# Edge loop on TensorE: a half's adjacency products before its weights, its scatter last

## The chip, the cores and the metric

The kernel runs on one core of a Trainium2 chip. The metric is the device time of one execution in microseconds (us); the median of three runs before the change is 2267.75 us (2266.25 to 2269.3).

## The reference, cut to what matters

The reference is two layers of a graph transformer over 1250 nodes of 512 features and 41250 edges (20000 in each direction and a loop at each node). The change lies in the stage that walks over the edges. For each edge, a small network turns 8 edge features into 512 weights (4 groups of 128), which multiply the features of the sending node and four edge attributes; the products are summed by receiving node. The second layer needs the adjacency matrix of the same edges.

```
tpw = h @ W_mlp4 / sqrt(64)              # h: hidden activations of the edge network
w1, w2, w3, w4 = jnp.split(tpw, 4, axis=-1)
s0 = x0[sender]; s1 = x1[sender]
y0 = edge_attrs[:, 0:1]; y1 = edge_attrs[:, 1:4]
p1 = w1 * s0 * y0
p2 = (w2 * s0)[:, :, None] * y1[:, None, :]
p3 = w3[:, :, None] * s1 * y0[:, None, :]
p4 = w4 * jnp.einsum('eum,em->eu', s1, y1) / SQRT3
msg0 = segment_sum(concatenate([p1, p4]), receiver)
msg1 = segment_sum(concatenate([p2, p3]), receiver)
...
out = segment_sum(h[src] * norm[:, None], dst)   # second layer: degree-normed adjacency times h
```

## The kernel before, in words

**Stages.** Everything is written out by hand, engine by engine, with semaphores between the engines; no scheduler moves anything. First come the edge network's hidden layers and the dense parts (to about 235 us of the span), then the edge loop (to about 856 us), then the expert network and the second layer.

**Blocks and halves.** Edges are sorted by receiver. The 1250 nodes are cut into 45 blocks (`NB`) of 28 nodes. A block takes one pass here, and a pass has four halves (`HALVES`, q = 0 to 3) of 2 x 128 edges: 45 x 4 = 180 halves. A half n does this:

- SyncE (SP) loads the hidden activations (L833) and the edge records (L843: indices and attributes of its 256 edges) four halves ahead. `record_load` waits until `hot_y`, `hot_low` and `hot_step` of half n have been built from the old record in that buffer (lines 838 to 842) before it loads the record of half n+4. L841 is its wait on `step_ready`, L842 that on `hot_y_ready`.
- GpSimd (POOL) builds `hot_y` of half n (L1071), then gathers the sender rows of half n+2 from DRAM with two indirect DMAs (L1041). Before these it waits for the record of half n+2 (`record_loaded`).
- VectorE (DVE) builds the one-hot tiles `hot` and `hot_low` (L1709, L1712), then multiplies the weights in PSUM by the gathered rows in three instructions (L1720, L1721, L1722); the last one increments `products_done`. Once a block it also turns the finished adjacency columns of an earlier block (L1698).
- ScalarE (ACT) builds `hot_step` of half n with two activations (L1243), the last of which increments `step_ready`. At a block's end it first waits for the last half's `scatter_done`, copies the block's two PSUM accumulators out (L1250 the messages, L1252 the adjacency), and only then builds the first `hot_step` of the next block; in between stands `block_start` (L1231) for the block after.
- TensorE (PE) runs per half, in this order: wait for `products_done` of n; weights of half n+2, four 64-row matmuls (`tile_weights`, L2367), the last of which increments `weights_done`; wait for `hot_y`; 20 scatter matmuls into the messages' PSUM bank, 10 for each of two groups of 128 edges (L2397); wait for `hot_low` and `hot_step`; two adjacency matmuls into the adjacency's bank (L2408), the last of which increments `scatter_done`.

Banks for messages and adjacency exist twice, for even and odd blocks, and are zeroed at a block's start by two matmuls (L2383, L2384). The order of TensorE's work is that of the Python code in `block_work`. ScalarE's order at a block's end is

```
s = block_steps_of(i * 2 + 1, 1)     # hot_step of the block's four halves
block_store(i * 2, 0)
block_start(i * 2 + 2, 0)
block_flush(i, 1, s)                 # waits for scatter_done of the last half
s = block_steps_of(i * 2 + 2, 0)
```

and the wait of a record's load is

```
sp.wait_ge(hot_low_ready, s * 4 + q + 1)
sp.wait_ge(step_ready, s * 4 + q + 1)
```

Of the kernel before, what the change touches and what calls it, by code (L numbers as in the profile page):

```python
# [44 lines left out]
def graph_block_kernel(nc, A, out):  # L45
# [6 lines left out]
    MUL = A["L0_gnn_W_up0"].shape[0]  # L52
# [33 lines left out]
    with ctx:  # L86
# [3 lines left out]
        def sem(name):  # L90
            return ctx.enter_context(nc.semaphore(name))
# [174 lines left out]
        hot_y = [edge_space2.take(2 * Y * GRAIN).rearrange("p (j y n) -> p j y n", j=2, y=Y) for q in range(HALVES)]  # L266
        hot_low = [edge_space2.take(P).bitcast(BF16).rearrange("p (j n) -> p j n", j=2) for q in range(HALVES)]
        hot_step = [edge_space2.take(NT * STEPS).bitcast(BF16).rearrange("p (j a n) -> p j a n", j=2, a=NT) for q in range(HALVES)]
# [20 lines left out]
        msg_psum = [psum[:, k, 0:3 * MUL] for k in range(2)]  # L289
        adj_psum = [psum[:, 2 + k, 0:NT * STEPS] for k in range(2)]  # L290
# [83 lines left out]
        hot_low_ready = sem("hot_low_ready")  # L374
        step_ready = sem("step_ready")
# [330 lines left out]
        def block_units(eng, b):  # L706

            return eng.value_load(span[0:1, 1, bass.ds(b, 1)], min_val=1, max_val=EDGE_UNITS)
# [11 lines left out]
        def next_step(eng, step):  # L720

            eng.reg_add(step, step, 1)
            return eng.snap(step, min_val=1, max_val=NB * EDGE_UNITS)
# [1433 lines left out]
        def _(pe):  # L2157
# [207 lines left out]
            def tile_weights(q):  # L2365
                for j in range(2):
                    last = nc.tensor.matmul(tile_w[q % 2][:, j, :], h3_slot[q][halves[j], :], w_mlp4[halves[j], :], start=True, stop=True)  # L2367
                last.then_inc(weights_done, 1)
# [7 lines left out]
            bands = [slice(g * GRAIN, (g + 1) * GRAIN) for g in range(4)]  # L2376
            step = step_counter(pe, "pe_step")

            def block_work(b, k):
                units = block_units(pe, b)  # L2380
                pe.wait_ge(msg_flushed, b + 1)
                pe.wait_ge(adj_flushed, b + 1)
                nc.tensor.matmul(msg_psum[k], zeros16[:, 0:P], zeros16[:, 0:3 * MUL], start=True, stop=False, skip_group_check=True)  # L2383
                nc.tensor.matmul(adj_psum[k], zeros16[:, 0:P], zeros16[:, 0:NT * STEPS], start=True, stop=False, skip_group_check=True)  # L2384
                with pe.Fori(0, units) as u:
                    s = next_step(pe, step)
                    for q in range(HALVES):
                        ahead = (q + 2) % HALVES
                        pe.wait_ge(products_done, s * 4 + q + 5)
                        pe.wait_ge(half_loaded[ahead], s * 16 + (q + 2) // HALVES * 16)  # L2390
                        tile_weights(ahead)
                        pe.wait_ge(hot_y_ready, s * 4 + q + 5)
                        for j in range(2):
                            p = prod[q][:, j, :, :]

                            def scatter(g, y, cols, of):
                                nc.tensor.matmul(msg_psum[k].rearrange("p (c u) -> p c u", u=MUL)[bands[g], cols, :],  # L2397
                                                 hot_y[q][:, j, y, :], p[:, of, :], start=False, stop=True, skip_group_check=True)

                            scatter(3, 0, slice(0, 3), slice(5, 8))  # L2400
                            scatter(0, 1, slice(0, 2), slice(1, 3))
                            scatter(1, 2, slice(0, 2), slice(1, 4, 2))
                            scatter(2, 3, slice(0, 2), slice(1, 5, 3))
                            scatter(0, 0, slice(2, 3), slice(0, 1))
                        pe.wait_ge(hot_low_ready, s * 4 + q + 5)
                        pe.wait_ge(step_ready, s * 4 + q + 5)
                        for j in range(2):
                            last = nc.tensor.matmul(adj_psum[k], hot_low[q][:, j, :], hot_step[q][:, j, :, :].rearrange("p a n -> p (a n)"),  # L2408
                                                    start=False, stop=True, skip_group_check=True)
                        last.then_inc(scatter_done, 1)  # L2410

            with pe.Fori(0, NB // 2) as i:
                for k in range(2):
                    block_work(i * 2 + k, k)
            block_work(NB - 1, 0)

            def transposes(key, pieces):
# [20 lines left out]
            for key in chain_order():  # L2438
# [9 lines left out]
                elif key[0] == "msgT1":  # L2448
# [4 lines left out]
                    for m, i in enumerate((1, 4, 6)):  # L2453
                        last = nc.tensor.matmul(out_b[:, D - P:], parts[i], ident[:, :], start=(m == 0), stop=(m == 2))
                    last.then_inc(full, 1)
                elif key[0] == "degree":
                    pe.wait_ge(consts_ready, 4 + NT - 1)
                    out_b, full = claim(pe, key)
                    for t in range(NT):
                        last = nc.tensor.matmul(out_b[:, t:t + 1], adj_sum[:, tile_cols[t]], ones_col[:, :], start=True, stop=True)  # L2460
# [4 lines left out]
                elif key[0] == "router_bias":  # L2465
# [3 lines left out]
                    for c in range(C):  # L2469
                        last = nc.tensor.matmul(out_b[:, 0:EX], routers_T[:, c, EX + PARTS + 1:EX + PARTS + 2].to_broadcast([P, P]),  # L2470
                                                routers_T[:, c, 0:EX], start=(c == 0), stop=(c == C - 1))
                    last.then_inc(full, 1)
                elif key[0] == "logits":
                    drained(pe, ("hT", key[1]))
                    out_b, full = claim(pe, key)
                    for c in range(C):
                        last = nc.tensor.matmul(out_b[:, 0:EX], xn_T[:, c, tile_cols[key[1]]], routers_scaled[:, c, :],
                                                start=(c == 0), stop=(c == C - 1))
                    last.then_inc(full, 1)
                else:  # L2480
# [5 lines left out]
                    def chunk(i):  # L2486
                        return msg_T[:, t % 2, i * P:i * P + P]

                    for c, (i0, i1) in enumerate(((0, 7), (4, 1), (5, 2), (6, 3))):
                        w = w_out[:, min(c, 1), :, :]  # L2490
                        nc.tensor.matmul(out_b[:, c * P:c * P + P], chunk(i0), w[:, 0, :], start=True, stop=False)
                        last = nc.tensor.matmul(out_b[:, c * P:c * P + P], chunk(i1), w[:, 1, :], start=False, stop=True)
# [8 lines left out]
                             start=False, stop=True, skip_group_check=True).then_inc(full, 1)  # L2501
# [22 lines left out]
            with pe.Fori(0, EX // 2) as i:  # L2524
                bounds = expert_bounds(pe, i)
                for a in range(2):
# [3 lines left out]
                    with pe.Fori(lo, hi) as t:  # L2530
# [14 lines left out]
                        for f in range(FC):  # L2545
                            pe.wait_ge(gelu_done, t * FC + f + 1)
                            for c in range(C):
                                last = nc.tensor.matmul(psum[:, f % UP_BANKS, 0:P], ew1[a][:, c, f * P:f * P + P], tile_T[:, c, :],  # L2548
                                                        start=(c == 0), stop=(c == C - 1))
# [13 lines left out]
            for s in range(NT):  # L2563
# [7 lines left out]
                for t, (out_b, full) in enumerate(open_banks):  # L2571
                    last = nc.tensor.matmul(out_b, adj_in[0:r, s, tile_cols[t]], z_lo[0:r, s, :], start=False, stop=(s == NT - 1))
# [34 lines left out]
            for f in range(HC):  # L2607
                pe.wait_ge(split_lo, lo_no["gw1", f])
                w_hi, w_lo = gw1_hi[f % 2], gw1_lo[:, :, f * P:f * P + P]
                for g, (g0, w) in enumerate(COLS):  # L2610
                    out_b, full = claim(pe, ("h1T", f, g))
                    for c in range(C):
                        for k, (lhs, rhs) in enumerate(((w_hi, ah_hi), (w_hi, ah_lo), (w_lo, ah_hi))):
                            last = nc.tensor.matmul(out_b[:, 0:w], lhs[:, c, :], rhs[:, c, g0:g0 + w],  # L2614
                                                    start=(c == 0 and k == 0), stop=(c == C - 1 and k == 2))
                    last.then_inc(full, 1)
            for t in range(NT):
                out_b, full = claim(pe, ("y2", t))
                pe.wait_ge(split_lo, lo_no["h1", t])
                for c in range(HC):  # L2620
                    if t == 0:
                        pe.wait_ge(split_lo, lo_no["gw2", c])
                    for k, (lhs, rhs) in enumerate(((h1_hi, gw2_hi[:, c, :]), (h1_lo, gw2_hi[:, c, :]), (h1_hi, gw2_lo[c][:, 0, :]))):
                        last = nc.tensor.matmul(out_b, lhs[:, t % 2, c, :], rhs,  # L2624
                                                start=(c == 0 and k == 0), stop=(c == HC - 1 and k == 2))
# [5 lines left out]
            for m in range(C):  # L2631
                pe.wait_ge(split_lo, lo_no["wk", m])
                w_hi, w_lo = w_k_hi[m], w_qk_lo[:, :, D + m * P:D + m * P + P]
                for g, (g0, w) in enumerate(COLS):
                    out_b, full = claim(pe, ("kT", m, g))
                    for c in range(C):
                        for k, (lhs, rhs) in enumerate(((w_hi, xn_hi), (w_hi, xn_lo), (w_lo, xn_hi))):
                            last = nc.tensor.matmul(out_b[:, 0:w], lhs[:, c, :], rhs[:, c, g0:g0 + w],
                                                    start=(c == 0 and k == 0), stop=(c == C - 1 and k == 2))
# [10 lines left out]
            for t in range(NT):  # L2650
                out_b, full = claim(pe, ("ek", t))
                r = rows(t)
                for c in range(C):
                    last = nc.tensor.transpose(out_b[0:r, c * P:c * P + P], ek_T[:, c, t * P:t * P + r], ident[:, :])
# [5 lines left out]
            for c in range(C):  # L2660
                for t in range(NT):
                    r = slice(0, rows(t))
                    last = nc.tensor.matmul(out_b[:, c * P:c * P + P], vx_rows[r, t, c * P:c * P + P],
                                            ek_rows[r, t, c * P:c * P + P], start=(t == 0), stop=(t == NT - 1))
# [36 lines left out]
            for key in ffn_order():  # L2701
# [7 lines left out]
                elif key[0] == "down":  # L2709

                    _, g, j = key
# [5 lines left out]
                    for k, (h, w) in enumerate(((shid_hi, w2_hi), (shid_lo, w2_hi), (shid_hi, w2_lo))):  # L2717
                        for i, (out_b, full) in enumerate(outs):
                            last = nc.tensor.matmul(out_b, h[0:r, g % 2, j, i * P:i * P + P], w[0:r, j % 2, :],  # L2719
                                                    start=(j == 0 and k == 0), stop=(j == SC - 1 and k == 2))  # L2720
# [10 lines left out]
                if key == ("route",):  # L2731
                    for c in range(C):
                        last = nc.tensor.matmul(out_b[0:1, 0:PARTS], mean_col[:, c:c + 1], routers_T[:, c, EX:EX + PARTS],
                                                start=(c == 0), stop=(c == C - 1))
                elif key == ("expert_w",):
                    nc.tensor.matmul(out_b[:, 0:SE], ones_col[0:1, :].to_broadcast([1, P]), expert_w[:, 0, :], start=True, stop=True)
                    last = nc.tensor.matmul(out_b[0:SE, SE:SE + 1], expert_w[:, 0, :], ones_col[0:1, :], start=True, stop=True)
                elif key == ("b2_mix",):
                    last = nc.tensor.matmul(out_b, expert_w_col[:, :].to_broadcast([SE, P]), expert_b2[0:SE, :], start=True, stop=True)
# [20 lines left out]
```

## Time and profile before

| | us |
|---|---|
| median of 3 runs (lowest, highest) | 2267.75 (2266.25, 2269.3) |
| time of the profiled execution | 2266.87 |
| its span, first to last instruction | 2264.9 |
| edge loop, 235 to 856 us | 621 |
| TensorE busy in all | 2060.1 (91%) |
| mean granted clock of TensorE | 0.972 |

The profile gives for each engine when each instruction ran and what it waited for. `PE` is TensorE's matmuls, `PEld` its weight loads, `SPq`, `ACTq` and `POOLq` are what the sequencers of those engines issue. A note in square brackets is the idle time of the engine before the instruction and what ended it; "issue" means that the profile shows no releaser. A matmul's end is modelled.

### The profile page before, as it was taken

To read this page: it belongs to the slowest core of one execution; us is meant where nothing else is said; L and a number is where in the kernel's file an instruction comes from. 1 tells how busy PE (TensorE), PEld (TensorE's weight loads), DVE (VectorE), ACT (ScalarE), POOL (GpSimd) and SP (SyncE) were. 2 spreads that over 40 slices of the span, in tenths; PEclk is the share of its full clock that TensorE was granted. 3 is DMA by queue.
4 is the path that set the end of the run, shared out by engine and by line. 5 is a ranking of instruction groups with operands and counts; after the bars stand their busy time and mean duration, and the time that the engine had idled before them with its cause. 6 is when DMAs were issued, how large, how long until landed. Compare 5 with 4: busy or idle time off the path is not lost.

```text
span 2264.9 us, 45107 instructions
## 1 busy us (share of the span) xinstructions
PE 2060.1 (91%) x13564; PEld 1487.3 (66%) x13565; DVE 1335.5 (59%) x2849; ACT 1040.0 (46%) x2316; POOL 618.2 (27%) x739
## 2 busy tenths in 40 slices
PE   7899888888888888799999999999599999889998
PEld 4444344344434337588888888888388888768886
DVE  3212788889888876655555555555612346664444
ACT  6531333333333332277777777777143223354443
POOL 2102677778777774300000000002100000000000
PEclk9999999999999998699999999999799999989999
DMA  6642566667676678355603420042700200310000
GB/s 217 220 164 85 151 188 186 188 185 191 187 190 190 181 210 317 136 194 197 260 19 117 156 79 19 19 167 85 260 10 10 84 19 19 107 43 10 10 10 18
DMA packets 157291, 288.52 MB, mean 127 GB/s; under 512 B 43533, under 2 KB 85270, under 8 KB 152615
## 3 DMA queue, kind: packets, MB, share of 16 engines
q1 hardware_dynamic: 111349, 158.80, 20.4%
q0 software_dynamic: 37552, 121.91, 18.7%
q10 hardware_dynamic: 8322, 6.89, 0.9%
q8 instruction: 44, 0.72, 0.1%
q14 instruction: 24, 0.20, 0.0%
HBM read 233.69 MB, written 53.85 MB: 127 GB/s over the span
## 4 chain that ended last, share of the span: by engine, by line
PE 60%; DVE 13%; issue 10%; DMA 9%; POOL 3%; ACT 3%; DVEq 1%; POOLq 1%; ACTq 0%; SPq 0%
PE psum L2548 14%; DMA big_b<-sender_table,wide 7%; PE psum L2686 6%; PE psum L2719 4%; PE psum L2538 4%; PE psum L2539 3%; PE psum L2540 3%; PE psum L2584 3%; PE psum L2593 3%; PE psum L2624 3%; PE psum L2614 2%; POOL big_b L1041 2%; DVE big_b L1721 2%; DVE big_b L1722 2%; PE psum L2266 2%
## 5 line engine op out<-in xcount | busy, mean ns | idle before, releaser
L1041 POOL DMA_INDIRECT big_b<-sender_table,wide x360 | 368.5, 1024 | 117.0 <-issue 84.2
L2397 PEld LDWEIGHTS psum<-big_b,wide 128*32 128x32 f32 x3600 | 166.2, 109 | 195.9 <-issue 134.3
L2367 PE MATMUL psum<-w_mlp,wide 64*128 64x512 f32 x728 | 206.9, 645 | 81.4 <-DVE big_b L1722 78.2
L2548 PEld LDWEIGHTS psum<-xn_T,big_b 128*128 128x128 f32 x2048 | 261.9, 191 | 21.1 <-issue 3.1
L2397 PE MATMUL psum<-big_b,wide 128*32 128x256 f32 (+2 forms) x3600 | 272.0, 390 | 0.8 <-POOL wide L1071 0.8
L2548 PE MATMUL psum<-xn_T,big_b 128*128 128x128 f32 x2048 | 265.0, 275 | 0.0
L1250 ACT ACTIVATE wide<-psum 128x384 f32<-128x384 f32 x45 | 22.1, 490 | 393.3 <-PE psum L2408 369.0
L1896 DVE TENSOR_TENSOR w_lo<-wide,w_hi 128x512 fp32r<-128x512 f32 x184 | 127.4, 692 | 117.9 <-ACT w_hi L1342 117.9
L2538 PE MATMUL psum<-w_hi,hid_hi 128*128 128x512 f32 x368 | 175.8, 478 | 9.5 <-DVE w_lo L1896 7.2
L1243 ACT ACTIVATE wide<-wide 128x290 bf16<-128x290 f32 x360 | 158.6, 527 | 41.9 <-PEq L2370 37.2
L1720 DVE TENSOR_TENSOR big_b<-psum,big_b 128x512 f32<-128x512 f32 x180 | 124.0, 689 | 84.8 <-DMA big_b<-sender_table,wide 70.6
L1722 DVE TENSOR_TENSOR big_b<-big_b,psum 128x768 f32<-128x768 f32 x180 | 170.3, 946 | 0.0
L1721 DVE TENSOR_TENSOR big_b<-big_b,psum 128x768 f32<-128x768 f32 x180 | 169.8, 943 | 0.0
L2686 PE MATMUL psum<-xn_T,wide 128*128 128x256 f32 (+1 forms) x640 | 154.7, 388 | 2.9 <-ACT shid_hi L1530 2.9
L1119 POOL DMA_DIRECT2D xn_T<-tokens_sorted x23 | 12.5, 542 | 529.0 <-PE psum L2518 529.0
L1342 ACT ACTIVATE w_hi<-wide 128x512 fp32r<-128x512 f32 x184 | 115.8, 629 | 71.0 <-PE psum L2540 71.0
L2539 PE MATMUL psum<-w_hi,hid_lo 128*128 128x512 f32 x368 | 146.0, 397 | 0.0
L2367 PEld LDWEIGHTS psum<-w_mlp,wide 64*128 64x128 f32 x728 | 55.6, 185 | 136.9 <-issue 77.0
L2540 PE MATMUL psum<-w_lo,hid_hi 128*128 128x512 f32 x368 | 144.4, 392 | 0.0
L1366 ACT ACTIVATE xn_T<-psum,table 128x128 f32<-128x128 f32 x368 | 130.1, 353 | 25.5 <-PE psum L2548 25.4
L2686 PEld LDWEIGHTS psum<-xn_T,wide 128*128 128x128 f32 (+1 forms) x640 | 123.9, 195 | 23.4 <-issue 4.0
L2548 PEld LDWEIGHTS psum<-xn_T,big_a 128*128 128x128 f32 x896 | 120.6, 200 | 21.2 <-issue 13.3
(453 smaller groups left out, 3949.8 us busy)
## 6 DMA issues: line engine op xcount, KB each, us to landing
big_a<-in_L_ffn_W SPq DMA_DIRECT2D x12, 2048.0 KB, 13.9
big_b<-in_L_ffn_W SPq DMA_DIRECT2D x12, 2048.0 KB, 13.7
wide<-in_L_ffn_W SPq DMA_DIRECT2D x8, 2048.0 KB, 23.5
wide<-edge_hidden SPq DMA_DIRECT2D x182, 64.0 KB
edge_hidden<-wide SPq DMA_DIRECT2D x21, 512.0 KB, 3.1
tokens_sorted<-zeros SPq DMA_DIRECT2D x29, 256.0 KB
adj_dram<-big_a SPq DMA_DIRECT2D x1, 6400.0 KB, 23.5
xn_T<-tokens_sorted POOLq DMA_DIRECT2D x25, 256.0 KB, 2.9
```

Of the source, the lines that this page charges most:

```text
L1041: nc.gpsimd.indirect_dma_start(out=sent[q][:, j, :], out_offset=None, in_=sender_table, in_offset=bass.IndirectOffsetOnAxis(ap=indices[j], ...
L1243: last = nc.scalar.activation(hot_step[q][:, j, :, :], block_steps[k], ACT.Sign, bias=record[q][:, j, Y + 1:Y + 2])
L1366: last = nc.scalar.activation(dst[:, f % HID_SLOTS, :], psum[:, f % UP_BANKS, 0:P], ACT.Gelu, bias=expert_bias_T[:, bass.ds(i * (2 * FC) + ...
L1721: nc.vector.tensor_tensor(prod[q][:, :, 5:8, :], s1, w[:, :, 2:3, :].to_broadcast([P, 2, 3, MUL]), ALU.mult)
L1722: nc.vector.tensor_tensor(prod[q][:, :, 2:5, :], s1, w[:, :, 3:4, :].to_broadcast([P, 2, 3, MUL]), ALU.mult)\
L2367: last = nc.tensor.matmul(tile_w[q % 2][:, j, :], h3_slot[q][halves[j], :], w_mlp4[halves[j], :], start=True, stop=True)
L2397: nc.tensor.matmul(msg_psum[k].rearrange("p (c u) -> p c u", u=MUL)[bands[g], cols, :], hot_y[q][:, j, y, :], p[:, of, :], start=False, st ...
L2538: nc.tensor.matmul(psum[:, Y_BANK, :], hid_hi[:, h, :], w2_hi[:, w, :], start=(f == 0), stop=False)
L2539: nc.tensor.matmul(psum[:, Y_BANK, :], hid_lo[:, h, :], w2_hi[:, w, :], start=False, stop=False)
L2540: nc.tensor.matmul(psum[:, Y_BANK, :], hid_hi[:, h, :], w2_lo[:, w, :], start=False, stop=(f == FC - 1))\
L2548: last = nc.tensor.matmul(psum[:, f % UP_BANKS, 0:P], ew1[a][:, c, f * P:f * P + P], tile_T[:, c, :], start=(c == 0), stop=(c == C - 1))
L2686: last = nc.tensor.matmul(out_b[0:r, 0:n], sw1_cols[:, c, j * P:j * P + r], xn_T[:, c, n0:n0 + n], start=(c == 0), stop=(c == C - 1))
```

## The change

TensorE's half has another order: the two adjacency matmuls come first, with their waits for `hot_low` and `hot_step`; then the wait for the products, the weights of half n+2, and the scatter. `scatter_done` is incremented by the last scatter matmul.

```diff
                     for q in range(HALVES):
                         ahead = (q + 2) % HALVES
+                        pe.wait_ge(hot_low_ready, s * 4 + q + 5)
+                        pe.wait_ge(step_ready, s * 4 + q + 5)
+                        for j in range(2):
+                            nc.tensor.matmul(adj_psum[k], hot_low[q][:, j, :], hot_step[q][:, j, :, :].rearrange("p a n -> p (a n)"),
+                                                    start=False, stop=True, skip_group_check=True)
                         pe.wait_ge(products_done, s * 4 + q + 5)
                         pe.wait_ge(half_loaded[ahead], s * 16 + (q + 2) // HALVES * 16)
                         tile_weights(ahead)
...
-                            scatter(0, 0, slice(2, 3), slice(0, 1))
-                        pe.wait_ge(hot_low_ready, s * 4 + q + 5)
-                        pe.wait_ge(step_ready, s * 4 + q + 5)
-                        for j in range(2):
-                            last = nc.tensor.matmul(adj_psum[k], hot_low[q][:, j, :], hot_step[q][:, j, :, :].rearrange("p a n -> p (a n)"),
-                                                    start=False, stop=True, skip_group_check=True)
+                            last = scatter(0, 0, slice(2, 3), slice(0, 1))
                         last.then_inc(scatter_done, 1)
```

TensorE at the beginning of a block's first half, behind the zeroing of the banks. Before (L2408 adjacency, L2367 weights, L2397 scatter, L2389 and L2390 the sequencer's register work for the waits):

```order
L2390 REGISTER_ALU [waits products_done]
L2367 MATMUL psum<-w_mlp,wide 128x512 [waits half_loaded2]
L2367 MATMUL psum<-w_mlp,wide 128x512
L2397 MATMUL psum<-big_b,wide 32x384 [waits hot_y_ready]
L2397 MATMUL psum<-big_b,wide 32x256 x3
...
L2408 MATMUL psum<-wide 128x290 [waits step_ready,hot_low_ready]
L2408 MATMUL psum<-wide 128x290
L2389 REGISTER_ALU
L2367 MATMUL psum<-w_mlp,wide 128x512 [waits half_loaded3,products_done]
```

The same place now (L2392 adjacency, L2402 scatter):

```order
L2392 MATMUL psum<-wide 128x290 [waits step_ready,hot_low_ready]
L2392 MATMUL psum<-wide 128x290
L2395 REGISTER_ALU [waits products_done]
L2367 MATMUL psum<-w_mlp,wide 128x512 [waits half_loaded2]
L2367 MATMUL psum<-w_mlp,wide 128x512
L2402 MATMUL psum<-big_b,wide 32x384 [waits hot_y_ready]
L2402 MATMUL psum<-big_b,wide 32x256 x3
...
L2389 REGISTER_ALU
L2392 MATMUL psum<-wide 128x290 [waits step_ready,hot_low_ready]
L2392 MATMUL psum<-wide 128x290
L2367 MATMUL psum<-w_mlp,wide 128x512 [waits half_loaded3,products_done]
```

The weights and the scatter of a block's first half now stand behind the wait for `step_ready`, which only the adjacency had before. The cycle of the three kinds of work is the same; a half's piece of it begins with the adjacency.

TensorE at a block's end, in the fourth half:

```order
+L2402 MATMUL psum<-big_b,wide 32x256 x3
+L2402 MATMUL psum<-big_b,wide 32x128
 L2385 REGISTER_ALU
 L2385 COMPARE_AND_BRANCH
```

The last work of a block was the adjacency pair of L2408; it is now the scatter, and `scatter_done` comes with its last matmul. The rows of the other four engines stand as before.

## Rows read from the trace of the kernel before

**Rows 1.** Edge loop: us; busy of PE, PEld, DVE, ACT, POOL; PEclk, DMA share, GB/s

```profile
235.00:856.00 621.00, 539.84 (x4768) 248.63 (x4768) 531.45 (x1121) 211.89 (x487) 482.02 (x578) 0.99 0.69 187
```

**Rows 2.** Edge loop, who waited for whom: us in total, times, longest

```profile
DVE big_b L1720 <- DMA big_b<-sender_table,wide: 70.6, 97, 5.9
...
DVE big_b L1720 <- PE psum L2367: 12.9, 15, 1.1
POOL wide L1071 <- DVE wide L1712: 11.5, 24, 1.3
```

**Rows 3.** Timeline of two blocks' ends: start us, us, what, [idle before]

```profile
506.06 1.13 PE L2367 MATMUL psum<-w_mlp,wide 64*128 64x512 f32 x4 [0.82 <-DVE big_b L1722]
...
507.12 1.49 PE L2397 MATMUL psum<-big_b,wide 128*32 128x384 f32 x20
...
508.55 0.42 PE L2408 MATMUL psum<-wide 128*128 128x290 bf16 x2
...
509.09 0.49 ACT L1250 ACTIVATE wide<-psum 128x384 f32<-128x384 f32 x1 [8.05 <-PE psum L2408]
...
509.77 0.96 ACT L1243 ACTIVATE wide<-wide 128x290 bf16<-128x290 f32 x2
...
510.32 1.13 PE L2367 MATMUL psum<-w_mlp,wide 64*128 64x512 f32 x4 [0.95 <-DVE big_b L1722]
...
511.05 0.34 SPq L843 DMA_DIRECT2D wide<-edge_records  x1
...
514.71 0.69 DVE L1720 TENSOR_TENSOR big_b<-psum,big_b 128x512 f32<-128x512 f32 x1 [0.80 <-DMA big_b<-sender_table,wide]
...
515.81 1.03 POOL L1041 DMA_INDIRECT big_b<-sender_table,wide  x1 [0.64 <-issue]
...
518.17 0.62 POOL L1071 TENSOR_TENSOR wide<-wide 128x256 f32<-128x256 f32 x1
...
518.95 1.03 POOL L1041 DMA_INDIRECT big_b<-sender_table,wide  x1 [0.16 <-issue]
...
521.31 0.63 POOL L1071 TENSOR_TENSOR wide<-wide 128x256 f32<-128x256 f32 x1
...
523.14 0.49 ACT L1250 ACTIVATE wide<-psum 128x384 f32<-128x384 f32 x1 [9.14 <-PE psum L2408]
...
524.00 0.96 ACT L1243 ACTIVATE wide<-wide 128x290 bf16<-128x290 f32 x2
```

**Rows 4.** Edge loop, SyncE's own waits

```profile
SPq L841 <- ACT wide L1243: 127.6, 44, 5.5
```

**Rows 5.** Chain of waits of 495 to 530 us: start us, us, what

```profile
497.94 3.94 DMA wide<-edge_records
```

**Rows 6.** Timeline of POOL, first and last gather that a record held up

```profile
258.68 1.03 POOL L1041 DMA_INDIRECT big_b<-sender_table,wide  x1 [2.88 <-DMA wide<-edge_records]
...
827.09 1.03 POOL L1041 DMA_INDIRECT big_b<-sender_table,wide  x1 [0.43 <-issue]
```

**Rows 7.** Copies at blocks' ends on ACT, the first and last of them; weights after one

```profile
442.11 0.49 ACT L1250 ACTIVATE wide<-psum 128x384 f32<-128x384 f32 x1 [8.31 <-PE psum L2408]
...
442.29 1.13 PE L2367 MATMUL psum<-w_mlp,wide 64*128 64x512 f32 x4
...
455.31 0.49 ACT L1250 ACTIVATE wide<-psum 128x384 f32<-128x384 f32 x1 [7.94 <-PE psum L2408]
...
L1250 ACT ACTIVATE wide<-psum x45: 490/490/491, 249.2 to 855.3; 128x384 f32<-128x384 f32 x45
```

**Rows 8.** Timeline of TensorE where it waits for nothing, a half's end

```profile
276.03 0.42 PE L2408 MATMUL psum<-wide 128*128 128x290 bf16 x2
276.38 1.13 PE L2367 MATMUL psum<-w_mlp,wide 64*128 64x512 f32 x4
```

**Rows 9.** The one adjacency pair that waited for hot_step

```profile
253.27 0.96 ACT L1243 ACTIVATE wide<-wide 128x290 bf16<-128x290 f32 x2 [3.30 <-issue]
...
254.38 0.41 PE L2408 MATMUL psum<-wide 128*128 128x290 bf16 x2 [0.50 <-ACT wide L1243]
```

More of the change, by code:

```diff
@@ L2396, in scatter @@
                             def scatter(g, y, cols, of):
-                                nc.tensor.matmul(msg_psum[k].rearrange("p (c u) -> p c u", u=MUL)[bands[g], cols, :],
-                                                 hot_y[q][:, j, y, :], p[:, of, :], start=False, stop=True, skip_group_check=True)
+                                return nc.tensor.matmul(msg_psum[k].rearrange("p (c u) -> p c u", u=MUL)[bands[g], cols, :],
+                                                        hot_y[q][:, j, y, :], p[:, of, :], start=False, stop=True, skip_group_check=True)
                             scatter(3, 0, slice(0, 3), slice(5, 8))
```

## The prediction

> **What bounds the kernel now.** Read the busy times by stage first, since the change touches one stage [rows 1]: the edge loop takes 621 us, 13.8 us for each of its 45 blocks. VectorE is busy for 531 us of it, TensorE for 540, GpSimd for 482. No engine is full, so the waits come next [rows 2]: VectorE's products wait 70.6 us for gathered rows and only 12.9 us for TensorE. TensorE is thus mostly not what others wait for. GpSimd sets a pace of its own: its `hot_y` instructions stand 3.14 us apart where nothing holds it up (518.17 and 521.31 in [rows 3]), and 180 x 3.14 = 565 us. Some 56 us of the stage lie above that pace.
>
> Then look for what holds GpSimd up. The gather at 515.81 [rows 3] comes 0.64 us after the last work where the next but one comes after 0.16 (518.95). The chain of waits names a record's load, 3.94 us from its issue [rows 5], and the first and last gathers of the kind stood for 2.88 and 0.43 us [rows 6]. Counted in the timeline between them, in the third half of a block, 31 gathers start just 0.86 us after their record has landed; they wait 22.8 us in all beyond the usual 0.16. That record is the one that SyncE may load only when ScalarE has built `hot_step` of the block's first half: SyncE waits on it 44 times, once a block, 127.6 us in sum [rows 4]. And ScalarE builds it only after the copies of the last block, which wait for TensorE's last `scatter_done`. So one thing that TensorE does is on the path: the end of a block's last half. In [rows 3]: adjacency done at 508.55 + 0.42 = 508.97, copy at 509.09, `hot_step` done at 509.77 + 0.96 = 510.73, record issued at 511.05. It lets through the gather at 515.81, for products two halves further on.
>
> **The change, part by part.**
>
> *`scatter_done` earlier.* Weights begin at 506.06, the scatter ends at 507.12 + 1.49 = 508.61, the adjacency at 508.97 [rows 3]. With the adjacency done while TensorE waits for the products, `scatter_done` comes 0.36 us earlier after the same weights; I take 0.35. In the first three halves nobody waits for it: it is asked for four halves later. At a block's end it moves the copy, `hot_step` and the record's load. The 31 waits above can shrink by 0.35 each or by all they are. The 16 that are longer than 0.35 give 16 x 0.35 = 5.6 us, the 15 shorter ones 2.0 us in sum, 7.6 us together. The 2.0 I don't count: GpSimd's other wait, for VectorE's `hot_low` (24 times, 11.5 us [rows 2]), stands in just the blocks where the record is nearly in time, and takes over. The rest of the blocks (14 of 45) gain nothing, as the record is early there.
>
> *Adjacency before the weights: work.* Nothing is added: 2 adjacency, 4 weight and 20 scatter matmuls a half, in the same cycle. The least that TensorE needs for a half is 2.84 us: 508.55 - 506.06 = 2.49 to the adjacency [rows 3], and 276.38 - 276.03 = 0.35 from it to the next weights [rows 8]. That stays. Where the products come every 3.1 us or more, the adjacency lies in the wait before them and costs nothing.
>
> *Adjacency before the weights: the wait.* In a block's first half the weights now stand behind `hot_step`. Behind that wait are queued the weights of the third half and the scatter, and later `weights_done` and `scatter_done`. Before, weights began at 510.32, 0.41 us before `hot_step` was done (510.73). In a fast block it is more: the copy starts at 442.11 and weights at 442.29 [rows 7], and `hot_step` is done 1.64 after the copy's start as above, 1.5 us behind the weights. Now they begin after it: 0.15 us until the adjacency starts (253.27 + 0.96 = 254.23, then 254.38 [rows 9]) and 0.35 us more. VectorE does not feel that at once. Weights begun at 510.32 are read at 514.71 [rows 3], and need 1.13; the slack is 514.71 - 510.32 - 1.13 = 3.3 us in a slow block, about 1 us less in a fast one, against a delay of 0.5 less the 0.35 gained, and up to 1.5 more: at most 1.7.
>
> But TensorE now has a chain of its own once a block: copies and `hot_step`, 0.12 + (510.73 - 509.09) = 1.76 us, in every other block 0.12 + (524.96 - 523.14) = 1.94; wake and adjacency, 0.15 + 0.35 = 0.50; three halves, 3 x 2.84 = 8.52; weights to scatter's end, 508.61 - 506.06 = 2.55. The sum is 13.33 or 13.51 us a block, 13.4 in the mean. No block can be shorter. Now the copies stand 455.31 - 442.11 = 13.20 us apart in a fast block [rows 7] and 523.14 - 509.09 = 14.05 in a slow one [rows 3]. Of the 44 distances between the first copy and the last [rows 7], 23 are below the new floor. Raising each to it costs 3.3 us in all, the largest by 0.34.
>
> *End of the loop.* The last half also ends 0.35 us earlier. That is less than the roundings above and is left in them.
>
> **The sum.** -5.6 + 3.3 = -2.3 us. Made against the profiled execution (2266.87 us, its span 2264.9 and 2.0 around it) that is 2264.6; the profiled execution lies 0.9 us below the median of 2267.75, so the median goes to **2265.4**. About 0.2% (4.5 us) is what a measurement of this kernel can tell from no change, and this is below.
>
> **The ends of the unknown costs.** What a record's load gains by being issued 0.35 us earlier no row shows: it waits among the gathers' packets (DMA share 0.69 [rows 1]). It may land no earlier at all (0 instead of -5.6) or in front of a gather, and then the waits could go in full (-22.8). I stay near 0.35, as the other engines' cycles keep their distances. What a second wait in the middle of TensorE's queue costs lies between nothing and the 0.15 us of [rows 9], and I take nothing, since the semaphores of three halves in four are long set.
>
> **The rivals.**
>
> 1. *TensorE's chain becomes the bound: slower.* The mechanism is the block's chain above, at the adjacency pair of the first half. For it: fast blocks are already 0.1 to 0.3 below the new floor, and a block with a floor has no means to catch up for one that was late. Against it: 13.4 is still below the mean of 13.8. If each half costs 0.1 us more than 2.84, by a wake like that of [rows 9], the floor is 13.8; 33 blocks, now at 13.4 in the mean, rise by 0.4, which is +13.2, less 5.6: +8, 2276. It decides from a floor of about 13.5 in the mean, where the lifts reach 5.6 us.
> 2. *The records' waits go, and more: faster.* The whole 7.6 us come, with few blocks lifted, or loads land well before the gathers' packets: -5 to -8, 2260 to 2263. For it: the waits are the largest stall that the change can touch. Against it: the time from `scatter_done` to the gather is 6.8 us, and 0.35 is a twentieth of it; a shorter block meets the floor of 13.4 next.
> 3. *TensorE's clock falls at the new pause: slower.* TensorE would stand idle for up to 1.7 us once a block. The granted clock was 0.99 over the stage, at the upper of its levels (2.4 GHz), though weights such as those at 510.32 had waited 0.95 us for their products [rows 1, 3]. At the lower level (1.2 GHz) one half a block at twice 2.84 would be 45 x 2.84 = +128 us at most. The Trainium skill, "TensorE: Matmul & The Clock Gate", section "HAM oscillation — how this bites in real kernels", says that pauses between bursts of matmuls which repeat each turn of a loop can drop the engine to its slower clock every turn. By it the sum would be that of this rival; the trace's 0.99 speaks against pauses of this size doing so.
> 4. *Nothing on the path moves.* Loads land when they did, and lifts are hidden: within 1 us of now. This is inside the likeliest case.
>
> **How the numbers follow.** The likeliest is that the two terms nearly cancel, between -4.5 and +4.5 us: 0.54. Rival 1 beyond +4.5 has 0.23, rival 2 beyond -4.5 has 0.21, rival 3 has 0.02. The range must leave out no more than 2 in 10: it takes in rival 2 to -8 (2260) and rival 1 to +8 (2276).
>
> **What would show it.** In the changed profile, SyncE's wait on `hot_step` falls by some 44 x 0.35 = 15 us from 127.6; ScalarE's copies follow the scatter line instead of the adjacency; the adjacency pair of a block's first half waits for ScalarE, 1 us or more, in most blocks; copies are never less than 13.3 us apart; the long distances (14.0) shrink. VectorE's wait for TensorE's weights stays near 13 us. The forecast is wrong if that wait grows by several us, if copies stand 13.6 or more apart in the fast blocks, if the gathers' waits for records vanish, or if the stage's clock falls below 0.99.

## The result, and the profile after

| us | before | changed |
|---|---|---|
| median (lowest, highest) | 2266.28 (2261.2, 2269.3), 8 runs | 2273.02 (2271.13, 2276.62), 8 runs |
| profiled execution | 2266.87 | 2273.28 |
| its span | 2264.9 | 2271.3 |
| last copy of a block's messages | 855.29 | 861.82 |
| TensorE's part of the chain that ended last | 60% | 78% |

The changed kernel takes 1.0034 of the time before, with a 95% interval of 1.0023 to 1.0045: it is slower by 7 us. That lies inside the range, but the forecast was a gain too small to be measured. Of the 6.4 us by which the span grew, all lie in the edge loop: 861.82 - 855.29 = 6.5.

The stage and a block's start within it, in the changed kernel (us; busy of PE, PEld, DVE, ACT, POOL; PEclk, DMA share, GB/s):

```profile
235.00:862.00 627.00, 542.73 (x4766) 248.70 (x4766) 532.02 (x1121) 211.37 (x486) 482.02 (x578) 0.98 0.69 185
515.00:527.00 12.00, 11.17 (x104) 5.34 (x104) 10.40 (x22) 3.78 (x9) 9.63 (x12) 1.00 0.77 207
527.00:529.50 2.50, 0.74 (x7) 0.24 (x4) 2.50 (x7) 2.02 (x5) 2.01 (x3) 1.00 0.43 116
529.50:533.00 3.50, 3.50 (x21) 1.42 (x22) 2.40 (x6) 2.85 (x7) 2.67 (x3) 0.54 0.79 203
```

The first line answers to [rows 1]: VectorE and GpSimd do the same work as before, in 6 us more. The other three are one block's start: TensorE at full clock, then almost idle, then at a granted clock of 0.54, the lower level (1.2 GHz).

The waits in the changed kernel (us in total, times, longest), answering to [rows 2] and taken over the same stretch, 240 to 855 us:

```profile
ACT wide L1250 <- PE psum L2402: 384.6, 44, 13.0
...
PE psum L2392 <- ACT wide L1243: 71.8, 44, 5.1
DVE big_b L1720 <- DMA big_b<-sender_table,wide: 68.5, 97, 2.0
...
DVE big_b L1720 <- PE psum L2367: 16.0, 17, 2.4
POOL big_b L1041 <- DMA wide<-edge_records: 13.5, 10, 2.1
...
POOL wide L1071 <- DVE wide L1712: 11.2, 22, 1.6
...
PE psum L2367 <- DVE big_b L1722: 2.8, 6, 0.9
```

Two lines of the same view of the kernel before stand against them:

```profile
PE psum L2367 <- DVE big_b L1722: 76.1, 103, 5.8
...
POOL big_b L1041 <- DMA wide<-edge_records: 5.0, 3, 2.9
```

TensorE used to wait for VectorE's products, 103 times and 76.1 us. Now it does so 6 times for 2.8 us, and in 44 blocks of 45 its adjacency pair waits for ScalarE's `hot_step` instead. The gathers' waits for a record's load went from 5.0 us in 3 places to 13.5 in 10; they were to shrink. The view puts only part of these waits down to the load. Counted in the timeline as in the prediction, beyond the usual 0.16 us before the gather of a block's third half, they went from 22.8 us to 29.9.

SyncE's own waits, answering to [rows 4]:

```profile
SPq L841 <- ACT wide L1243: 142.7, 44, 5.3
...
SPq L832 <- PE psum L2367: 30.5, 43, 3.0
```

The wait on `hot_step` rose from 127.6 us by 15 where the forecast had it fall by 15, and SyncE has a new one, for TensorE's weights (L832). The timeline of one block's start (start us, us, what, [idle before]) answers to [rows 3]:

```profile
526.64 0.60 PE L2402 MATMUL psum<-big_b,wide 128*32 128x256 f32 x4
...
527.34 0.29 PE L2384 MATMUL psum<-zeros 128*128 128x290 bf16 x1
...
527.42 0.49 ACT L1250 ACTIVATE wide<-psum 128x384 f32<-128x384 f32 x1 [8.46 <-PE psum L2402]
...
528.28 0.97 ACT L1243 ACTIVATE wide<-wide 128x290 bf16<-128x290 f32 x2
...
529.39 0.41 PE L2392 MATMUL psum<-wide 128*128 128x290 bf16 x2 [1.76 <-ACT wide L1243]
...
529.73 2.05 PE L2367 MATMUL psum<-w_mlp,wide 64*128 64x512 f32 x4
...
531.71 2.21 PE L2402 MATMUL psum<-big_b,wide 128*32 128x384 f32 x20
531.82 0.69 DVE L1720 TENSOR_TENSOR big_b<-psum,big_b 128x512 f32<-128x512 f32 x1 [1.10 <-PE psum L2367]
...
534.19 1.08 POOL L1041 DMA_INDIRECT big_b<-sender_table,wide  x1 [1.70 <-DMA wide<-edge_records]
```

Read it as a ring. The last scatter ends at 526.64 + 0.60 = 527.24 and releases the copy at 527.42; ScalarE finishes `hot_step` at 528.28 + 0.97 = 529.25; the adjacency starts at 529.39, the weights at 529.73, and from there TensorE works through four halves to the next last scatter. In this block the clock had fallen to the lower level as well, so the weights took 2.05 us where they take 1.13. How closely the ring holds the loop is seen in the copies (L1250) in the timeline of ScalarE, answering to [rows 7]:

```profile
446.66 0.49 ACT L1250 ACTIVATE wide<-psum 128x384 f32<-128x384 f32 x1 [8.47 <-PE psum L2402]
...
460.21 0.49 ACT L1250 ACTIVATE wide<-psum 128x384 f32<-128x384 f32 x1 [8.29 <-PE psum L2402]
...
487.13 0.49 ACT L1250 ACTIVATE wide<-psum 128x384 f32<-128x384 f32 x1 [8.20 <-PE psum L2402]
...
500.50 0.49 ACT L1250 ACTIVATE wide<-psum 128x384 f32<-128x384 f32 x1 [8.46 <-PE psum L2402]
...
514.04 0.49 ACT L1250 ACTIVATE wide<-psum 128x384 f32<-128x384 f32 x1 [8.28 <-PE psum L2402]
...
542.60 0.49 ACT L1250 ACTIVATE wide<-psum 128x384 f32<-128x384 f32 x1 [9.86 <-PE psum L2402]
```

460.21 - 446.66 = 13.55; 500.50 - 487.13 = 13.37; 514.04 - 500.50 = 13.54; 527.42 - 514.04 = 13.38; 542.60 - 527.42 = 15.18, the block with the low clock. Of the 40 distances between the third copy and the 43rd, 34 are 13.37, 13.38, 13.54 or 13.56, none is shorter, and four are 15.2. Before, 17 of these 40 were below 13.35 and the least was 13.16.

### The profile page after: what moved, and what is told of

Read it like the earlier page. It is cut to its first block, busy times and chain, and to the rows that moved or that the text cites. A ratio compares the mean times of both kernels' runs of the same rounds, so it can differ in the third digit from the quotient of the medians.

```text
span 2271.3 us, 45107 instructions
## 1 busy us (share of the span) xinstructions
PE 2063.6 (91%) x13564; PEld 1487.2 (65%) x13565; DVE 1336.1 (59%) x2849; ACT 1040.0 (46%) x2316; POOL 618.5 (27%) x739
## 4 chain that ended last, share of the span: by engine, by line
PE 78%; DVE 8%; issue 5%; ACT 4%; DMA 3%; ACTq 1%; POOL 1%; DVEq 0%; POOLq 0%; SPq 0%
PE psum L2548 14%; PE psum L2402 10%; PE psum L2367 7%; PE psum L2686 6%; PE psum L2719 4%; PE psum L2538 4%; PE psum L2539 3%; PE psum L2540 3%; PE psum L2584 3%; PE psum L2593 3%; PE psum L2624 3%; PE psum L2614 2%; PE psum L2392 2%; DMA big_b<-sender_table,wide 2%; PE psum L2266 2%
## 5 line engine op out<-in xcount | busy, mean ns | idle before, releaser
L2402 PEld LDWEIGHTS psum<-big_b,wide 128*32 128x32 f32 x3600 | 167.5, 110 | 199.1 <-issue 112.5
L2402 PE MATMUL psum<-big_b,wide 128*32 128x256 f32 (+2 forms) x3600 | 274.1, 393 | 0.0
L2367 PE MATMUL psum<-w_mlp,wide 64*128 64x512 f32 x728 | 210.4, 656 | 10.9 <-DVE big_b L1722 9.1
L1250 ACT ACTIVATE wide<-psum 128x384 f32<-128x384 f32 x45 | 22.1, 490 | 399.8 <-PE psum L2402 399.8
L2392 PE MATMUL psum<-wide 128*128 128x290 bf16 x360 | 75.9, 292 | 71.8 <-ACT wide L1243 71.8
```

The costliest lines, as they stand in the source:

```text
L2402: return nc.tensor.matmul(msg_psum[k].rearrange("p (c u) -> p c u", u=MUL)[bands[g], cols, :], hot_y[q][:, j, y, :], p[:, of, :], start=Fa ...
```

## The experiments

The theory after the result: the adjacency pair ahead of a block's first weights closes the ring above, and that costs more than the earlier `scatter_done` brings. This is theory A of the expectations. Its rivals: the other three halves cost something too, by their new order (B); or the ring is harmless and the fallen clock is the whole loss (C). Each kernel was run against the kernel before in the same session. **Session one** was unlike the others: the kernel before took 2297.79 us in it, and in the kernels profiled there ScalarE began its copies up to 2.4 us after the last matmul of a block, where it is 0.12 us behind an adjacency pair or 0.17 behind a scatter elsewhere. I therefore repeated three of its four kernels.

**Which halves carry it.** `q123` does the adjacency first in the second to fourth half and last in a block's first half, so `scatter_done` comes early at the block's end but nothing stands behind `hot_step` at its start. `q0` is the opposite: the adjacency first in a block's first half alone.

```diff
+                        def adjacency():
+                            pe.wait_ge(hot_low_ready, s * 4 + q + 5)
+                            pe.wait_ge(step_ready, s * 4 + q + 5)
...
+                        if q in (1, 2, 3):
+                            adjacency()
                         pe.wait_ge(products_done, s * 4 + q + 5)
...
                             last = scatter(0, 0, slice(2, 3), slice(0, 1))
+                        if q not in (1, 2, 3):
+                            last = adjacency()
                         last.then_inc(scatter_done, 1)
```

(`q0` has `(0,)` in place of `(1, 2, 3)`.)

> The adjacency stands first in halves 2 to 4 of a block and last, behind the scatter, in the first half. Theory A (the changed kernel is slower because the weights of a block's first half stand behind hot_step, which hangs on TensorE's own last scatter: a ring of 13.36 or 13.56 us that no block can undercut): the ring is open, scatter_done of the last half stays early, the distances between copies fall below 13.36 again, and the time is 1 to 5 us below the kernel before, 2261 to 2265. Theory B (an adjacency ahead of the weights costs something in each half): three quarters of the loss stay, about 2271. Theory C (only the clock that falls in the pause at a block's start costs): no pause, no fall, 2266.

> The adjacency stands first in a block's first half alone; in halves 2 to 4 all is as before the change, scatter_done behind the adjacency. Theory A: the ring is closed and holds the same work, so blocks last 13.36 or 13.56 us at least and the time is that of the changed kernel, 2272 to 2275. Theory B: a quarter of the loss, about 2268. Theory C: the pause at a block's start is as long as in the changed kernel, so about as many falls of the clock and 2272 or so.

Measured in session one: `q123` 2294.27 us, ratio 0.9988 (0.9961 to 1.0015); `q0` 2326.74, ratio 1.0124 (1.0092 to 1.0155). The wait at a block's start costs by itself, some 29 us there, and the other three halves cost nothing. How much they gain that session could not tell. Nor does it say how much of the 29 us is the ring: with copies released late the pauses at the blocks' starts in `q0` were up to 3.65 us long, and between its third copy and its 43rd the clock fell 17 times, against 6 in `q123`. `q0` was not run again.

**Zeros in the pause.** `fill` is the changed kernel with ten matmuls of zeros into the adjacency's bank behind the zeroing, so that TensorE is not idle while ScalarE works; the sums are not changed by them.

```diff
+                for _ in range(10):
+                    nc.tensor.matmul(adj_psum[k], zeros16[:, 0:P], zeros16[:, 0:NT * STEPS], start=False, stop=True, skip_group_check=True)
```

> The changed kernel with ten more matmuls of zeros added onto the cleared adjacency bank at each block's start, where TensorE stands idle. Theory C, and A with the clock as a term of its own: no fall of the granted clock in the loop's middle, the blocks of 15.2 us are gone, 4 x 1.64 = 6.6 us less: 2266 to 2268. If the clock is of no account: 2273 as it was. The blocks stay at 13.36 and 13.56 us by theory A; by B nothing changes.

Measured in session one: 2321.56 us, ratio 1.0101 (1.0068 to 1.0134), with six falls of the clock in the profile between the third copy and the 43rd. With copies released so late the ten matmuls did not cover the pause, and the question stayed open.

**`hot_step` ahead of the copies.** `act_after` is the changed kernel, but ScalarE builds the `hot_step` of the next block's first half before it waits for `scatter_done` and copies. It is written for one pass a block, which is what these edges need, and so it also takes ScalarE's loop over passes out; what that is worth by itself was not tried.

```diff
+            def block_first(b, k):
+                act.reg_mov(ended, step)
                 act.wait_ge(block_steps_ready, b + 1)
                 act.sem_inc(loop_entered, 1)
...
+                step_of(0, next_step(act, step), k)
+                return act.snap(ended, min_val=0, max_val=NB * EDGE_UNITS)
...
                 block_start(i * 2 + 2, 0)
+                s = block_first(i * 2 + 2, 0)
                 block_flush(i, 1, s)
```

> The changed kernel, but ScalarE builds hot_step of a block's first half before it copies the last block's sums out (written for one pass a block, which is what these edges need). Theory A: the ring is gone, and with it the record's wait behind the copies; the gathers' 22.8 us of waits for records mostly go, less what the next limit takes: 2250 to 2262. Theory B: at least some 5 us above what the kernel before would have with the same edit. Theory C: no pause, 2266 or less.

Measured in session one: 2253.19 us, ratio 0.9806 (0.9775 to 0.9838). The ring is open: the first `hot_step` no longer stands behind the copies, nor do TensorE and the records' loads. How much of the 44.6 us belongs to that session's late copies the third session shows.

**Session two** had the usual times (before: 2265.47). `after_b`, `q123_b` and `fill_b` are the changed kernel, `q123` and `fill` again; `act_before` is the kernel before with ScalarE's edit alone.

> The changed kernel once more, beside the others on one chip. Theory A (a ring through TensorE's own last scatter, ScalarE's copies and hot_step): slower than the kernel before by 7 us where ScalarE starts its copies 0.12 us after scatter_done, and by 20 to 30 us on a chip where ScalarE is released a microsecond later, since all of that lies on the ring. Theory B (an adjacency ahead of the weights costs something in each half): 7 us on any chip.

> Adjacency first in halves 2 to 4 alone, once more. Theory A: the ring is open, 0 to 5 us below the kernel before. Theory B: three quarters of the changed kernel's loss.

> Ten more matmuls of zeros at each block's start in the changed kernel, once more. If falls of the clock cost 1.64 us each on the ring: below the changed kernel by that times the falls that are spared (up to 6.6 us), blocks still never below 13.36 us. If the clock is of no account: as the changed kernel.

> The kernel before, but ScalarE builds hot_step of a block's first half before it copies the last block's sums out (written for one pass a block). Theory A: records no longer wait behind the copies, so 10 to 20 us below the kernel before, within 3 us of the same edit on the changed kernel, as TensorE's order then decides nothing. Theory B: 5 us or more below the changed kernel with the same edit.

| | us | ratio (95%) | against before |
|---|---|---|---|
| after_b | 2272.29 | 1.0036 (1.0021 to 1.005) | +6.8 |
| q123_b | 2253.39 | 0.9954 (0.9937 to 0.997) | -12.1 |
| fill_b | 2267.56 | 1.0011 (1.0 to 1.0021) | +2.1 |
| act_before | 2243.78 | 0.9908 (0.9892 to 0.9923) | -21.7 |

The change is the sum of two things of opposite sign. The adjacency first in the other three halves, and with it the earlier `scatter_done`, is worth -12.1 us (`q123_b`), twice what I had expected. The adjacency ahead of a block's first weights, put on top of that, costs 2272.29 - 2253.39 = 18.9 us. What it costs alone, on the kernel before, only `q0` of session one shows. In the waits of `q123_b` (us in total, times, longest) TensorE waits for products again and VectorE little for weights:

```profile
DVE big_b L1720 <- DMA big_b<-sender_table,wide: 67.0, 92, 4.8
PE psum L2367 <- DVE big_b L1722: 58.1, 107, 4.7
...
POOL wide L1071 <- DVE wide L1712: 14.5, 37, 0.7
...
DVE big_b L1720 <- PE psum L2367: 6.9, 8, 1.3
```

In `fill_b` the adjacency follows 0.53 us behind the zeros, as its timeline shows:

```profile
445.53 0.49 ACT L1250 ACTIVATE wide<-psum 128x384 f32<-128x384 f32 x1 [8.42 <-PE psum L2404]
445.58 1.40 PE L2386 MATMUL psum<-zeros 128*128 128x290 bf16 x10
...
447.50 0.41 PE L2394 MATMUL psum<-wide 128*128 128x290 bf16 x2 [0.53 <-ACT wide L1243]
...
459.07 0.49 ACT L1250 ACTIVATE wide<-psum 128x384 f32<-128x384 f32 x1 [8.29 <-PE psum L2404]
```

Between the third copy and the 43rd the clock fell nowhere, against four times in `after_b`, and 4.7 us came back (2272.29 - 2267.56). The ring stayed: 459.07 - 445.53 = 13.54, and no block is under 13.37. So of the 18.9 us about 4.7 are the clock and 14.2 the ring. The clock's part is that of falls beyond the usual: the kernel before and `q123_b` have one fall each in the same stretch of their profiles.

**Session three** (before: 2266.61) asked why the earlier `scatter_done` is worth so much: the moment of that signal at a block's end (called A1 in the expectations), or something else in the new order of the halves. `late` is `q123` with three matmuls of zeros at a block's end, ahead of `scatter_done`; they take about what the adjacency pair took. `q3` does the adjacency first in a block's last half alone.

```diff
+                        if q == HALVES - 1:
+                            for _ in range(3):
+                                last = nc.tensor.matmul(adj_psum[k], zeros16[:, 0:P], zeros16[:, 0:NT * STEPS], start=False, stop=True,
+                                                        skip_group_check=True)
                         last.then_inc(scatter_done, 1)
```

`act_after_b` is `act_after` again, and `act_q123` joins `q123` with ScalarE's edit.

> Adjacency first in halves 2 to 4, with three more matmuls of zeros (0.13 us each) between the last scatter of a block and its scatter_done: the signal comes about 0.35 us later again, as before the change, and no wait for hot_step stands before the weights. Theory A1 (the whole gain of the open-ring order is the earlier signal at a block's end): back to the kernel before, within 3 us, that is some 10 us above the order without the three matmuls. Theory A2 (the gain is that the adjacency lies in TensorE's wait for products in each half): still 8 us or more below the kernel before.

> Adjacency first in a block's last half alone. Theory A1 (only scatter_done of the last half is on a path): as with halves 2 to 4, some 12 us below the kernel before. Theory A2: a third of that, 4 us below.

> The changed kernel with ScalarE's hot_step of a block's first half ahead of its copies, once more. Theory A (the changed order costs only through the ring over ScalarE's copies): 20 us or more below the kernel before, within 3 us of the same edit on the kernel before, which took 21.7 off. Theory B (each half costs): 14 us below or less.

> Both edits that helped: ScalarE builds hot_step of the first half ahead of its copies, and the adjacency stands first in halves 2 to 4. With ScalarE's edit no record waits for scatter_done of the last half any more, so the earlier signal should bring nothing on top: 19 to 24 us below the kernel before. If it adds up, 34 below.

| | us | ratio (95%) | against before |
|---|---|---|---|
| late | 2270.05 | 1.0013 (1.0003 to 1.0023) | +3.4 |
| q3 | 2256.86 | 0.996 (0.9946 to 0.9973) | -9.8 |
| act_after_b | 2245.03 | 0.9906 (0.9892 to 0.9919) | -21.6 |
| act_q123 | 2244.93 | 0.9907 (0.9892 to 0.9922) | -21.7 |

`late` undoes all of the gain and `q3` alone brings most of it, so what counts is when the signal comes at a block's end. A rival for `late` is that its three matmuls hold up the weights behind them. Its profile speaks against it: VectorE's products wait for weights 7.2 us in 9 places, against 6.9 in 8 in `q123_b`. The traces of the kernels show by what way. The record that SyncE asks for in a block's first half took 2.99 us in the mean from issue to landing before, 2.54 in `q123_b` and 3.04 in `late` (in the loop's middle, from the third copy on); the gather behind it waited 0.48 us a block beyond the usual 0.16 before, 0.04 in `q123_b` and 0.61 in `late`. Over the whole loop these waits are 22.8, 6.0 and 29.5 us. By the signal the load is issued 0.3 us sooner (0.35 less the 0.05 by which the copy starts later behind a scatter); it also lands faster, and nearly the whole wait goes.

With ScalarE's edit TensorE's order decides nothing: 2243.78, 2245.03 and 2244.93 us for the order of before, the changed one and that of `q123`, and as the first stems from another session, by ratio to the kernel before 0.9908, 0.9906 and 0.9907. SyncE's own waits show why, in `act_before`:

```profile
SPq L842 <- POOL wide L1071: 92.6, 130, 2.2
SPq L841 <- ACT wide L1240: 52.5, 42, 4.0
```

The wait on `hot_step` is 52.5 us instead of 127.6 [rows 4], and the record is there in time however the block ends. A block's start in its timeline:

```profile
447.00 0.42 PE L2422 MATMUL psum<-wide 128*128 128x290 bf16 x2
...
447.55 0.49 ACT L1259 ACTIVATE wide<-psum 128x384 f32<-128x384 f32 x1 [6.94 <-PE psum L2422]
447.76 1.13 PE L2381 MATMUL psum<-w_mlp,wide 64*128 64x512 f32 x4
...
449.65 1.03 POOL L1041 DMA_INDIRECT big_b<-sender_table,wide  x1 [0.16 <-issue]
449.74 0.33 SPq L843 DMA_DIRECT2D wide<-edge_records  x1
...
452.81 1.04 POOL L1041 DMA_INDIRECT big_b<-sender_table,wide  x1 [0.16 <-issue]
...
456.00 1.04 POOL L1041 DMA_INDIRECT big_b<-sender_table,wide  x1 [0.16 <-issue]
```

Every first gather of a half stands only the usual 0.16 us here. The kernel before with ScalarE's edit beats both kernels: 21.7 us (0.9%) below before, 28.5 below the changed one. Where a block may take more than one pass, `q123` needs no such restriction and brings 12.

## Why the prediction was wrong

**What bounds the kernel: right.** `hot_step` of a block's first half, the record and its gather were the path, and taking `hot_step` out from behind the copies gives 21.7 us, close to the 22.8 us of waits counted there.

**The earlier `scatter_done`: right in mechanism and place, undersized.** I put 5.6 us on 16 waits shortened by 0.35 each, on the ground that a load issued sooner lands sooner by as much. It measured 12.1 (`q123_b`) and 9.8 (`q3`). Two steps fell short: the load also lands some 0.4 us faster, and the shorter waits, left out as taken over by VectorE's `hot_low`, went too (GpSimd's wait for it only grew from 11.5 to 14.5 us).

**The size of the ring: right.** Forecast 13.33 or 13.51 us a block, measured 13.37 or 13.54; the copy starts 0.17 us after the scatter, where I took 0.12.

**The cost of the ring: the step that failed.** "Of the 44 distances between the first copy and the last, 23 are below the new floor. Raising each to it costs 3.3 us in all." It measured 18.9. The floor was compared with the blocks of the kernel before, while the same sum took a gain in those blocks as well. The two exclude each other: a block held at 13.45 cannot be shortened by an earlier signal. With that signal and no ring the blocks take 13.26 us in the mean (`q123_b`). Raising its 40 distances between the third copy and the 43rd to 13.54 and 13.37 in turn costs 11.8 us by itself, in 35 of them. (The 3.3 itself is a little low: the 23 lifts of the kernel before sum to 3.6.) The rest of the 18.9 is the clock (4.7) and the loop's start, which the sum left out. Behind the first copy ScalarE issues seven loads and builds `hot_step` late:

```profile
253.09 1.39 ACT L1243 ACTIVATE wide<-wide 128x290 bf16<-128x290 f32 x3 [3.55 <-issue]
...
254.20 0.64 PE L2392 MATMUL psum<-wide 128*128 128x290 bf16 x2 [5.14 <-ACT wide L1243]
```

It did so before too, at 253.27 [rows 9], but the weights did not stand behind it. Now TensorE waits 5.14 us and its clock falls behind that; the first two distances sum to 33.1 us against 29.5 in `q123_b`, 3.6 more. The three pieces make 20.1, near enough to 18.9. Between the two profiles the last copy moved by 861.82 - 842.81 = 19.0 us. That the pieces add is argued from the distances, not tried.

**Rival 1 is what came**, with 0.23 on it: the ring became the bound and the time rose by 7. Its price was worked out wrongly too: it asked whether a half costs 0.1 us more, and put the turning point at a floor of 13.5. The floor of 13.45 was enough, since the kernel without it would have been well below.

**Rival 3, the clock, came in small.** It had 0.02. The prediction went by pauses of 0.95 us and a granted clock of 0.99 [rows 1, 3]. The kernel before had longer ones, though seldom, and its clock fell at 782.24 behind this one:

```profile
781.62 1.51 PE L2367 MATMUL psum<-w_mlp,wide 64*128 64x512 f32 x4 [2.11 <-DVE big_b L1722]
```

In the changed kernel TensorE pauses 1.76 us at every other block's start, and in the blocks between like this:

```profile
515.83 0.41 PE L2392 MATMUL psum<-wide 128*128 128x290 bf16 x2 [1.37 <-ACT wide L1243]
```

In four of the 40 blocks the clock fell to 1.2 GHz for 3.4 us, for +1.64 us each, and all four falls came behind a pause of 1.76 us. TensorE is the bound, so the loss is not caught up. The Trainium skill, "TensorE: Matmul & The Clock Gate", section "HAM oscillation — how this bites in real kernels", warns of pauses between bursts that repeat each turn of a loop and drop the clock each turn. The trace agrees with the direction only: one turn in ten, 4.7 us instead of 128.

**Signs to look for.** Right: the adjacency pair of a block's first half waits for ScalarE in 44 blocks, copies stand 13.28 us apart at the least, and VectorE's wait for weights stays near 13 (16.0). Wrong: SyncE's wait on `hot_step` grew by 15 us, the gathers' waits for records did not shrink, and nor did the long distances. Of the signs against the forecast one came, the stage's clock at 0.98.

**Left open.** Why copies were released up to 2.4 us late in session one wasn't tried further. Sessions one and three are on record with the same chip (12) and session two with another (4), so the chip alone does not explain it. Nor was why a load issued 0.3 us sooner lands faster.

## What to carry to other kernels

Work that is moved ahead takes its own waits with it, and everything behind it in the engine's queue then waits for them; follow each such wait back, and if it leads to the engine's own last signal, a ring has been closed and its length is the least time of a turn. Compare that length with the turn as it would be once the other parts of the change have paid, never with the turn of today. And before the waiting side is reordered, look at the releasing one: here two copies stood in front of the one instruction that three engines needed, and moving it ahead made the order on TensorE indifferent.

## What the runs showed of the hardware that was not expected

- TensorE's clock fell to the lower level in four of 40 blocks. A pause of 1.76 us stood ahead of 20 of them, these four included, and one of 1.32 to 1.38 us ahead of the others. Ten small matmuls of zeros (1.40 us) in the pause kept the clock up in all 40.
- The kernel before took 2297.79 us in one session and 2265.47 and 2266.61 in two others. In the kernels profiled in the first of these ScalarE was released 0.9 to 1.9 us in the mean after the semaphore's last matmul, and in three of them SyncE issued the record's load 0.51 to 0.57 us in the mean after `hot_step` was done, where it is 0.32 elsewhere. A kernel whose path leads through that release feels it (+32 us); with `hot_step` ahead of the copies it took 2253.19 there and 2245.03 elsewhere (+8).
- The same small load of a record took 2.3 us in the mean in `act_before` and 3.0 in `late`. The two issue it at different moments among the gathers.
